# Transposed attention scores without the masked quarter, in 32x64 tiles, with odd heads in reverse order

## What is computed

```
scores = einsum('bhqd,bhkd->bhqk', q, k) / 4
scores = where(allowed, scores, NEG)      # stage 1: key < query; stage 2: key <= query
out    = einsum('bhqk,bhkd->bhqd', softmax(scores, -1), v)
```

## Time and profile before

| What | us |
|---|---|
| median of 3 runs (lowest, highest) | 1501.13 (1499.71, 1501.81) |
| the profiled execution's own time | 1500.57 |
| its span, first to last instruction | 1498.8 |
| PE busy in the span | 1411.4 |
| DVE / ACT / POOL busy | 1104.7 / 897.5 / 863.2 |
| mean granted TensorE clock | 0.98 |

### The profile page before, as it was taken

The page is one execution under the profiler, slowest core; times in us unless marked ns, Lnnn a source line. Parts: engine busy times, 40 slices in busy tenths (PEclk is TensorE's granted clock), DMA queues, the critical chain, the costliest instruction groups (busy, mean ns, idle before and its releaser), DMA issues. The chain is left out here.

```text
span 1498.8 us, 57219 instructions
## 1 busy us (share of the span) xinstructions
PE 1411.4 (94%) x22238; PEld 1065.2 (71%) x22238; DVE 1104.7 (74%) x3057; ACT 897.5 (60%) x1541; POOL 863.2 (58%) x1184
## 2 busy tenths in 40 slices
PE   6999999999999999987999999999999769999997
PEld 4777777777777777765777777777777536666664
DVE  6777777777777777763677787878777658989896
ACT  2555655555555555543666666666666447777773
POOL 3555544555544555443578777777777735454543
PEclk9999999999999999997999999999999969999998
DMA  5500000000000000002000000000000000000001
GB/s 165 152 2 1 0 0 0 0 0 0 0 0 0 0 0 0 2 3 97 27 24 14 21 14 21 14 21 14 21 14 9 2 1 29 29 35 28 35 28 43
DMA packets 31207, 32.40 MB, mean 22 GB/s; under 512 B 3937, under 2 KB 29602, under 8 KB 31138
## 3 DMA queue, kind: packets, MB, share of 16 engines
q1 hardware_dynamic: 31138, 31.46, 6.7%
HBM read 23.06 MB, written 8.39 MB: 21 GB/s over the span
## 5 line engine op out<-in xcount | busy, mean ns | idle before, releaser
L1060 POOL TENSOR_SCALAR_AFFINE_SELECT a_probs_t<-a_probs_t 128x512 f32<-128x512 f32 x256 | 162.3, 669 | 62.3 <-ACT a_probs_t L709 62.2
L1595 DVE TENSOR_REDUCE c_neg_max<-score_banks 128x8 f32<-128x512 f32 (+1 forms) x128 | 116.5, 951 | 82.7 <-PE score_banks L1328 82.7
L1074 POOL TENSOR_TENSOR a_less<-a_attn,a_remote 128x512 f32<-128x512 f32 x32 | 40.8, 1275 | 217.8 <-DVE a_attn L884 217.8
L1736 POOL TENSOR_SCALAR_AFFINE_SELECT c_probs_t<-c_probs_t 128x512 f32<-128x512 f32 x256 | 153.9, 639 | 14.6 <-ACT c_probs_t L1522 14.1
L709 ACT ACTIVATE a_probs_t<-score_banks 128x2048 f32<-128x2048 f32 x64 | 120.2, 1878 | 46.9 <-PE score_banks L554 46.9
L397 PE MATMUL side_banks<-a_xn_t,a_w_qk 128*128 128x256 f32 x512 | 134.5, 398 | 1.6 <-ACT a_xn_t L654 0.7
L1522 ACT ACTIVATE c_probs_t<-score_banks 128x2048 f32<-128x2048 f32 x64 | 120.3, 1880 | 26.2 <-PE score_banks L1356 26.2
L861 DVE TENSOR_REDUCE a_neg_max<-score_banks 128x8 f32<-128x512 f32 (+1 forms) x128 | 116.3, 950 | 6.0 <-PE score_banks L524 6.0
L397 PEld LDWEIGHTS side_banks<-a_xn_t,a_w_qk 128*128 128x128 f32 x512 | 93.0, 196 | 13.1 <-issue 2.3
L2162 POOL TENSOR_TENSOR r_hn<-rz_t,half_hn 128x256 f32<-128x256 f32 x32 | 23.3, 730 | 123.2 <-ACT rz_t L1991 123.2
L664 ACT ACTIVATE a_k_z<-side_banks,a_b_k,row_half 128x256 f32<-128x256 f32 x128 | 61.8, 563 | 53.9 <-PE side_banks L397 53.9
(11 more groups left out here) (265 smaller groups left out, 3959.3 us busy)
## 6 DMA issues: line engine op xcount, KB each, us to landing
x_sb<-in_x SPq DMA_DIRECT2D x32, 256.0 KB, 3.0
ctx_in<-in_ctx SPq DMA_DIRECT2D x32, 256.0 KB, 2.7
out<-y SPq DMA_DIRECT2D x32, 256.0 KB, 2.1
w_ih<-in_ffn_w_ih SPq DMA_DIRECT2D x1, 768.0 KB, 5.3
w_hh<-in_ffn_w_hh SPq DMA_DIRECT2D x1, 768.0 KB, 6.2
a_raw_qk<-in_attn_qk_w SPq DMA_DIRECT2D x1, 512.0 KB, 3.7
a_raw_cross<-in_xattn_qk_w SPq DMA_DIRECT2D x1, 512.0 KB, 4.9
b_ih<-in_ffn_b_ih SPq DMA_DIRECT2D x1, 384.0 KB, 6.4
```

What stands on the lines that cost most here:

```text
L1060: nc.gpsimd.affine_select(out=probs, in_=probs, pattern=[[0, 4], [1, 128]], compare_op=ALU.is_ge, fill=0.0, base=-1, channel_multiplier=-1 ...
L1595: ins = nc.vector.tensor_reduce(neg_max[:, tt, :].rearrange("p (i s l) -> p i s l", i=4, s=2)[:, :, :, late], all_scores[:, :, :, 128 * (1 ...
L1736: nc.gpsimd.affine_select(out=heads, in_=heads, pattern=[[0, 4], [1, 128]], compare_op=ALU.is_ge, fill=0.0, base=0, channel_multiplier=-1) ...
```

## The change

In both attention stages the transposed scores are computed without the quarter of late keys and early queries. Each 128x128 matmul becomes two in 32x64 tiles: one with the 64 early keys against all 128 queries, one with the 64 late keys against the 64 late queries. For odd heads keys and queries stand in reverse order, so that their short half falls on the other column half of the array. For that the K projection of odd heads streams its tokens backwards, `scores` reads those keys back in the plain order, the queries are read backwards in `scores_t`, and `values` reads the weights of odd heads backwards. V of odd heads is projected from a reversed copy of the tokens, which ACT makes (`reverse`), so V is projected in two halves of the heads. The maxima are added by 32 matmuls instead of 16; the same matmuls write NEG into the quarter left out. The maxima are turned with a matmul by `turned` instead of a transposition by `ident_bf`. POOL's four masks now take every second head. Stage 2 has the same edits, with `ctx_t` and `ctx_rev`, 16 columns a head instead of 17, and base=0; they are not shown.

```diff
+        self.turned = sb("turned", [128, 128], BF16)
...
             def project(dst, e, first):
                 for c in range(C):
-                    mm = pe.matmul(dst[:, e * PT:e * PT + PT], w_qk[:, c, first + e, :], xn_t[:, c, :],
-                                   start=(c == 0), stop=(c == C - 1), skip_group_check=True)
+                    toks = xn_t[:, c, :].rearrange("p (t k) -> p t k", t=2)
+                    mm = pe.matmul(dst[:, e * PT:e * PT + PT], w_qk[:, c, first + e, :],
+                                   toks[:, :, ::-1] if first and e else toks, start=(c == 0), stop=(c == C - 1), skip_group_check=True)
                 return mm
...
             def project_v(at, tt):
                 if tt == 0:
+                    pe.wait_ge(reversed_, at.count(1, 1))
                     pe.wait_ge(k_ready, at.count(1, 1))
                     if at.off == 0:
                         pe.wait_ge(weights_made, 3)
                         pe.wait_ge(gates_step, 4)
                 else:
                     pe.wait_ge(q_ready, at.count(1, 1))
-                for c in range(C):
-                    mm = pe.matmul(v_bank[tt][:, 0:VW], xn_t[:, c, S * tt:S * tt + S], w_v[:, c, 0:VW],
-                                   start=(c == 0), stop=(c == C - 1), skip_group_check=True)
+                for e in range(2):
+                    for c in range(C):
+                        toks = (xn_rev if e else xn_t)[:, c, S * tt:S * tt + S]
+                        mm = pe.matmul(v_bank[tt][:, 0:VW].rearrange("p (h e n) -> p e h n", e=2, n=HD + 1)[:, e],
+                                       toks,
+                                       w_v[:, c, 0:VW].rearrange("p (h e n) -> p e h n", e=2, n=HD + 1)[:, e],
+                                       start=(c == 0), stop=(c == C - 1), skip_group_check=True)
                 mm.then_inc(v_filled, 1)
...
                 for late in range(2):
                     for e in range(2):
                         for i in range(4):
+                            keys = k_z[at.par][group(i), e, :, S * tt:S * tt + S]
                             mm = pe.matmul(near_far(half(e), i)[:, :, 128 * (1 - late):128 * (1 - late) + 64 * (1 + late)],
                                            q_f[at.par][group(i), e, S * tt + 64 * late:S * tt + 64 * late + 64],
-                                           k_z[at.par][group(i), e, :, S * tt:S * tt + 64 * (1 + late)],
+                                           (keys[:, :, ::-1] if e else keys)[:, :, 0:64 * (1 + late)],
                                            start=False, stop=True, skip_group_check=True)
...
-                pe.transpose(maxT_bank[:].bitcast(BF16)[:, 0:128], max_part[:, tt, :], ident_bf[:]).then_inc(maxT_filled, 1)
+                pe.matmul(maxT_bank[:, 0:128], max_part[:, tt, :], cross.turned[:], start=True, stop=True,
+                          skip_group_check=True).then_inc(maxT_filled, 1)
 
             def scores_t(at, tt):
                 if tt == 0:
                     pe.wait_ge(max_done, at.count(2, 2))
                 else:
                     pe.wait_ge(exp_done, at.count(2, 1))
-                toks = slice(S * tt, S * tt + S)
                 for j in range(4):
-                    for i in range(4):
-                        pe.matmul(slot(i, j), k_z[at.par][group(i), j // 2, j % 2, toks],
-                                  q_f[at.par][group(i), j // 2, toks], start=(j == 0), stop=False, skip_group_check=True)
+                    e = j % 2
+                    for late in range(2):
+                        rows, early, side = half(late ^ e), S * tt + 64 * late, late * (1 - e)
+                        for i in range(4):
+                            keys = k_z[at.par][group(i), e, j // 2, S * tt:S * tt + S][:, 64 * (late ^ e):64 * (late ^ e) + 64]
+                            queries = q_f[at.par][group(i), e, early:S * tt + S]
+                            pe.matmul(score_banks[rows, i, 128 * j + 64 * side:128 * j + 64 * side + 64 * (2 - late)],
+                                      keys, queries[:, ::-1] if e else queries,
+                                      start=(j == 0), stop=False, skip_group_check=True)
                 pe.wait_ge(maxT_ready, at.count(2, tt + 1))
                 for j in range(4):
-                    for i in range(4):
-                        by_row = score_banks[:, i, :].rearrange("p (e j r) -> p j e r", e=2, j=4)
-                        mm = pe.matmul(by_row[:, j], cross.slot_rows[group(i), j, :],
-                                       max_t[group(i), tt, :].rearrange("p (e r) -> p e r", e=2),
-                                       start=False, stop=True, skip_group_check=True)
+                    for h in range(2):
+                        for i in range(4):
+                            quarters = score_banks[half(h), i, :].rearrange("p (s b r) -> p s b r", s=2, r=64)[:, j // 2]
+                            mm = pe.matmul(quarters[:, 1:3, :] if j % 2 else quarters[:, 0::3, :], cross.slot_rows[group(i), j, half(h)],
+                                           max_t[group(i), tt, :].rearrange("p (e r) -> p e r", e=2),
+                                           start=False, stop=True, skip_group_check=True)
                 mm.then_inc(sct_filled, 1)
 
             def values(at, tt):
                     pe.wait_ge(av_ready, at.count(2, 1))
                 for h in range(H):
                     g, j = h // 4, h % 4
-                    slot_j = 2 * (j % 2) + j // 2
-                    if j == 0:
-                        pe.wait_ge(masked, at.count(8, 4 * tt + g + 1))
+                    if h % 8 == 0:
+                        pe.wait_ge(masked, at.count(8, 4 * tt + g + 2))
+                    probs = probs_t[tt][:, h, :]
                     mm = pe.matmul(av_bank[HW * j:HW * j + HW, 128 * g:128 * g + 128], v_heads[at.par][:, tt, h, :],
-                                   probs_t[tt][:, 4 * g + slot_j, :], start=True, stop=True, skip_group_check=True)
+                                   probs[:, ::-1] if j % 2 else probs, start=True, stop=True, skip_group_check=True)
                 mm.then_inc(av_filled, 1)
...
+            def reverse(at):
+                act.wait_ge(xnT_ready, at.count(1, 1))
+                wait(act, v_filled, at.count(2, 0))
+                nc.scalar.activation(xn_rev[:].rearrange("p c (t k) -> p (c t) k", t=2),
+                                     xn_t[:].rearrange("p c (t k) -> p (c t) k", t=2)[:, :, ::-1],
+                                     ACT.Copy).then_inc(reversed_, 1)
...
                     copy_max(prev, 0)
                 if at.real:
+                    reverse(at)
                     evac_k(at)
                 if prev.real:
                     exp(prev, 0)
...
+            for e in range(2):
+                turned = ident[:, 64 * e:64 * e + 64]
+                nc.vector.tensor_copy(cross.turned[:, 64 * e:64 * e + 64], turned[:, ::-1] if e else turned).then_inc(zeroed, 1)
+                early = cross.slot_rows[:, 0::2, 64 * (1 - e):64 * (1 - e) + 64]
+                nc.vector.tensor_scalar(early, early, cross.diagonal[:, 8 + e:9 + e], None, ALU.add).then_inc(zeroed, 1)
+                nc.vector.memset(max_part[64 * e:64 * e + 64, :, 8 + e::32], NEG).then_inc(zeroed, 1)
...
             def mask_weights(at, tt):
                 pool.wait_ge(exp_done, at.count(2, tt + 1))
                 pool.sem_inc(pool_turn, 1)
-                for g in range(4):
-                    probs = probs_t[tt][:, 4 * g:4 * g + 4, :]
-                    nc.gpsimd.affine_select(out=probs, in_=probs, pattern=[[0, 4], [1, 128]], compare_op=ALU.is_ge,
-                                            fill=0.0, base=-1, channel_multiplier=-1).then_inc(masked, 1)
+                for g in range(2):
+                    for e in range(2):
+                        four, sign = probs_t[tt][:, 8 * g + e:8 * g + 8:2, :], 1 - 2 * e
+                        nc.gpsimd.affine_select(out=four, in_=four, pattern=[[0, 4], [sign, 128]], compare_op=ALU.is_ge,
+                                                fill=0.0, base=-1, channel_multiplier=-sign).then_inc(masked, 1)
...
-            pool.wait_ge(ident_made, 1)
-            nc.gpsimd.tensor_copy(ident_bf[:], ident[:]).then_inc(ident_made, 1)
```

More of the change, by code:

```diff
@@ L1262, in project @@
                 for c in range(C):
-                    mm = pe.matmul(dst[:, e * PT:e * PT + PT], cross.w_qk[:, c, first + e, :], src[:, c, :],
-                                   start=(c == 0), stop=(c == C - 1), skip_group_check=True)
+                    toks = src[:, c, :].rearrange("p (t k) -> p t k", t=2)
+                    mm = pe.matmul(dst[:, e * PT:e * PT + PT], cross.w_qk[:, c, first + e, :],
+                                   toks[:, :, ::-1] if first and e else toks, start=(c == 0), stop=(c == C - 1), skip_group_check=True)
                 return mm
@@ L1281, in project_v @@
                     pe.wait_ge(q_ready, at.count(1, 1))
```

(19 more changed lines are left out.)

71 lines of the change are left out of this document (42 added, 29 removed).

## The result

The changed kernel takes **1545.93 us** (median of 4 runs, 1544.34 to 1546.65) against 1501.16 for the kernel before (1499.71 to 1501.81): ratio 1.0298, 95% interval 1.0280 to 1.0316. It is 45 us slower. The forecast was 1507.5, 6 us slower, with a range of 1472 to 1520, so the direction came true and the size did not.

What follows compares the result with a forecast made beforehand. The prediction took PE to bound both attention stages. Per pair, 0.12 us in stage 1 plus 0.08 in stage 2, times 32, added 6.4 us to 1500.57; with 0.56 for the median, 1507.5 us, range 1472 to 1520.

Steps and rivals of the forecast that it cites:

- The other edits on PE: V projection and transposition of the maxima on PE: +0.02 us per projection in stage 1, nothing in stage 2 or for the transposition.
- The block: Transposed scores plus maxima, twice a pair in both attention stages: +0.04 us each, bounds -0.27 and +0.10.
- The step (64 in flight, freed in order, 17 ns a matmul): PE's feed in the block: 64 instructions in flight, places returned in order, refilled at 17 ns per float32 matmul; +0.04 us a block.
- The V projection: Eight instruction pairs instead of four, same columns: four more gaps of about 5 ns, +0.02 us each in stage 1.
- A pair without a stall: Stage 1, one pair of sequences: two blocks at 0.04 and two projections at 0.02 us, 0.12 us more.
- Stage 2: One pair of sequences: two blocks at 0.04 us, 0.08 us more, with the projections costed at nothing.
- Backward reads, ACT's copy and POOL's masks: Both attention stages: backward matmul reads at ordinary speed, ACT's 0.6 us copy hidden in idle time, POOL's masks no added time.
- The upper bound's 0.26: Stage 1's share per pair, in us, of the upper bound 32 x (0.26 + 0.20) = +15 us.
- (a): Block rival: the feed does not bind, places being given back out of order; 1468 us, or some 1485; chance 0.27.
- (b): Block rival: feed and stream cancel within 0.2%, a block taking 1.24 us; 1502 us; chance 0.18.
- (c): V projection rival: slow PSUM writes in pieces of 16 or 17 words, 0.9 us more a projection; 1616 us; chance 0.05.
- The sum: Both attention stages: 32 x 0.20 = 6.4 us more, giving 1507.5 us; the forecast's own range 1504 to 1520.

Runs made afterwards that it cites:

- e12: e8 with every float32 matmul of the second scores cut to 64 queries, more left out than the mask allows, to time the block: 1493.00 us.
- e4: The changed kernel with the maxima added by 16 matmuls of 128 rows in each block instead of 32 of 64 rows: 1544.74 us.
- e9: The kernel before, its second scores leaving out the late 64 queries of each tile in both stages, to time the block: 1496.41 us.
- e14: e13 with the float32 matmuls of a block reordered, the 16 that stream 64 columns ahead of the 16 that stream 128: 1510.41 us.
- e13: e4 with 67 extra matmuls of 2 columns in the prologue of stage 1, so that its loop touches 7 instruction blocks: 1512.23 us.
- e1: The changed kernel with stage 1's loop written out as straight code on TensorE alone: 1621.61 us.
- e5: e1 with 32 extra matmuls of 2 columns in the prologue of stage 2, nothing in its loop: 1520.72 us.
- e2: The kernel before with stage 1's loop written out as straight code on TensorE alone: 1500.73 us.
- e8: e4 with the mask matmuls of both stages also as 8 of 128 rows instead of 16 of 64 rows: 1515.61 us.

## Why the prediction was wrong

- **The step that failed** is one that the prediction doesn't have. "The other edits on PE" and the block were costed by their time on the array; that the change adds 410 instructions to each turn of stage 1's loop on PE, and that the loop has to be held somewhere, was priced at nothing. In its place the runs showed that such a loop is read again in each turn, with a wait at every branch back: 12 x (3.16 - 0.24) = 35 us of the 45. Of these 26.1 are idle PE, and the other 9 agree with a mean clock of 0.98 over the 532 us of the loop. The row that could have warned was on the page of before: an instruction queue with 0.75 MB and stage 1 at 0 GB/s. A loop of 1485 instructions, 93 KB, was being kept, and the change makes it 118 KB. The range had no place for it either.
- **The block**, forecast 1.36 us: 1.36. The step (64 in flight, freed in order, 17 ns a matmul) is seen in the block itself, where the loads pause after 34 and go on 17 ns apart, and e12 lies in its range. It is not the whole of it: it would have had e4 at 1.25, e9 at 1.13 or less and e14 at 1.20 to 1.29. They took 1.37, 1.27 and 1.36, held by what I read as a wait between tile forms, the loads of weights and the stream. Right number, one of three limits named, and partly luck.
- **The V projection**: +0.02 forecast for each of the two of a pair in stage 1. The first didn't change (1.11 and 1.20 us in turn, before and after), the second took 0.04 to 0.05 more: together what was forecast.
- **A pair without a stall**: 0.12 us more forecast in stage 1; e13 shows 0.14, with its own form of the maxima. Stage 2: 0.08 forecast, after shows (30.28 - 30.13) / 2 = 0.08. Backward reads, ACT's copy and POOL's masks cost nothing visible, as forecast. The upper bound's 0.26 a pair of stage 1 is 0.24 by its own terms (2 x 0.10 + 2 x 0.02), which changes nothing here.
- **Rivals.** (a) and (b) fell with the block. (c), slow writes in pieces of 17 words, fell with the rows of L448. The Trainium skill ("SBUF — State Buffer", "Door 1: The DMA port swizzle") says that any non-contiguous access of PSUM slows matmuls significantly; the trace doesn't agree for these pieces, with at most 0.05 us more for a projection of 1.02.
- **The sum** without the stall would have held as to its range, 1504 to 1520: e13 took 1512.23. But it was 6.4 us over the kernel before against 10.9 measured, 16 x 0.28 + 16 x 0.22 = 8 of them in the turns. By the two traces 2.8 of the rest lie behind stage 2's loop, where the last pairs and the untouched stage 3 run; why wasn't tried. So the terms of the sum account for at most some 10 us of the 45, and the direction would have come true by them too.

The Trainium skill has rules that bear on this. "Runtime: NRT & Kernel Launch" (Instruction fetch mechanics) gives TensorE 128 KiB for instructions, filled in blocks of 16 KiB, with a stall where a branch goes to what isn't there. The runs agree as far as they go (packets of 16 KB; branches of 3.3 to 3.9 us), and add that 8 touched blocks are one too many. Both pages, the second being "Advanced Engine Details and Errata" (ISA Cache) of the Trainium skill, say that only two lines are kept; by that the loop of the kernel before would have been read again too. It was not (one turn of its stage 1, 207 to 248.2 us, has no packet of instructions), so the measurement decides. The prediction weighed neither, nor a loop's size at all.

## What to carry to other kernels

Count the instructions of an engine's loop body before adding to it: one that splits matmuls pays in instructions even where it saves columns. On TensorE a body that touched 8 blocks of 256 instructions was read again in each turn, at 3 to 9 us a turn, and one that touched 7 was not, so a few instructions ahead of the loop can be worth 100 us; the row of the instruction queue and the branch's duration show it at once. And before skipping part of a matmul's stream, ask whether the weight load beside it is as long.

## What was not expected of the hardware

- A loop's cost depends on where it begins: the same 1672 instructions had turns of 30.28 and 38.96 us. Why 7 blocks are kept and 8 are not stays open.
- If the body is read again, it is read whole: nine packets of 256 instructions for 1895. Instruction queue during one turn (170 to 214 us) of after:

```profile
q8 instruction: 9, 0.15, 1.5%
```

- The cost of a stall is more than its length: if a second wait follows (e1: 3.89 and 2.29 us), the granted clock goes to 0.50 for some 8 us, and a branch of 4.2 us costs 8.7 a turn.
- Code written out without a loop isn't free either: e5 has three pairs of stage 1 that take 1.6 to 3.5 us longer than others of their kind, e2 (with 22% fewer instructions) none.
- Where matmuls on 64 and on 128 columns of the array follow each other, the second group starts 0.09 (e8's masks) to 0.2 us (e4's maxima) later. That it waits for the tiles that the wider matmul covers is my reading.
